# First cross-attention of a Perceiver-style network: the short key chunk moved from first to last, and the weighting dealt out in another rhythm

## The reference, cut to what matters

```python
q = (input_q @ wq).reshape(B, LQ, 16, 64).transpose(0, 2, 1, 3)     # LQ = 128
k = (input_k @ wk).reshape(B, LK, 16, 64).transpose(0, 2, 1, 3)     # LK = 12544
v = (input_k @ wv).reshape(B, LK, 16, 16).transpose(0, 2, 1, 3)
attn = softmax(einsum('bhqd,bhkd->bhqk', q, k) / sqrt(64), axis=-1)
out = einsum('bhqk,bhkd->bhqd', attn, v)                            # x = x + out
```

## Time and profile before

| | |
|---|---|
| median of 3 runs | 954.5 us (953.8 to 955.16) |
| the profiled execution, its own time | 958.71 us |
| its span, first to last instruction | 956.9 us |
| mean granted TensorE clock | 0.989 |
| TensorE busy | 925.9 us, 97% |
| VectorE, ScalarE, GpSimd busy | 73%, 60%, 39% |

### The profile page before, as it was taken

The page is one execution under the profiler, slowest core; times in us unless marked ns, Lnnn a source line. Parts: engine busy times, 40 slices in busy tenths (PEclk is TensorE's granted clock), DMA queues, the critical chain, the costliest instruction groups (busy, mean ns, idle before and its releaser), DMA issues.

```text
span 956.9 us, 30568 instructions
## 1 busy us (share of the span) xinstructions
PE 925.9 (97%) x13321; PEld 723.9 (76%) x13321; DVE 695.4 (73%) x876; ACT 570.2 (60%) x1404; POOL 372.8 (39%) x406
## 2 busy tenths in 40 slices
PE   7999999999999999999999999878989999999998
PEld 5667777777777777777777777567978887889998
DVE  4588888888888888888888888845035654367886
ACT  5666666666666666666666666503246663346764
POOL 2544444444444444444444444302023331513332
PEclk9999999999999999999999999979989999999999
DMA  6101101100101101000101100069449897409992
GB/s 237 25 25 25 25 25 25 25 25 25 25 25 25 25 26 25 25 25 25 25 25 25 25 3 3 3 257 382 138 176 274 283 281 274 174 2 313 323 335 92
DMA packets 78554, 98.10 MB, mean 103 GB/s; under 512 B 21584, under 2 KB 56928, under 8 KB 78432
## 3 DMA queue, kind: packets, MB, share of 16 engines
q1 hardware_dynamic: 77344, 94.67, 30.6%
q10 hardware_dynamic: 1088, 1.57, 0.5%
HBM read 95.68 MB, written 0.13 MB: 100 GB/s over the span
## 4 chain that ended last, share of the span: by engine, by line
PE 81%; DVE 7%; ACT 5%; issue 4%; POOL 2%; DMA 1%; SPq 0%; DVEq 0%; POOLq 0%
PE ps L360 28%; PE ps L411 18%; PE ps L421 9%; PE ps L369 7%; PE ps L1586 6%; PE ps L1062 3%; PE ps L1603 2%; PE ps L1607 2%; PE ps L1604 2%; ACT x_pr L1228 2%; DVE c1T_lo L1266 1%; DVE x_negc L1272 1%; ACT c1T_hi L1222 1%; DVE x_negm L1275 1%; ACT x_prT L1236 1%
## 5 line engine op out<-in xcount | busy, mean ns | idle before, releaser
L671 DVE TENSOR_REDUCE x_peak<-ps 128x2 f32<-128x1024 f32 (+1 forms) x200 | 239.5, 1205 | 90.3 <-PE ps L411 81.8
L587 ACT ACTIVATE probs<-ps,x_peak 128x512 f32<-128x512 f32 (+1 forms) x400 | 265.5, 693 | 49.8 <-DVE x_peak L671 49.5
L690 DVE STREAM_TRANSPOSE probsT<-probs 128x1024 f32<-128x1024 f32 (+1 forms) x200 | 225.5, 1183 | 2.8 <-ACT probs L587 2.8
L411 PE MATMUL ps<-keys,qT 64*32 64x512 f32 (+1 forms) x3200 | 216.9, 586 | 1.3 <-ACT probs L587 0.7
L574 ACT COPY keys<-ps 128x512 f32<-128x512 f32 (+1 forms) x200 | 113.3, 580 | 149.9 <-PE ps L360 149.9
L421 PEld LDWEIGHTS ps<-probsT,vals 64*32 64x32 f32 x6016 | 115.3, 106 | 94.0 <-issue 93.2
L859 POOL TENSOR_SCALAR vals<-vals_t,x_side 128x512 f32<-128x512 f32 (+1 forms) x100 | 151.9, 1536 | 51.6 <-PEq L429 51.6
L360 PE MATMUL ps<-ctxT_hi,wk_hi 128*128 128x512 f32 (+1 forms) x400 | 157.3, 393 | 0.0
L360 PE MATMUL ps<-ctxT_hi,wk_lo 128*128 128x512 f32 (+1 forms) x400 | 154.2, 386 | 0.0
L360 PE MATMUL ps<-ctxT_lo,wk_hi 128*128 128x512 f32 (+1 forms) x400 | 154.2, 386 | 0.0
L421 PE MATMUL ps<-probsT,vals 64*32 64x128 f32 x6016 | 131.9, 271 | 0.0
(11 more groups left out here) (252 smaller groups left out, 1304.8 us busy)
## 6 DMA issues: line engine op xcount, KB each, us to landing
m_w<-in_m_w SPq DMA_DIRECT2D x32, 1024.0 KB, 7.7
ctx_raw<-in_ctxT SPq DMA_DIRECT2D x24, 512.0 KB, 3.7
ctx_two<-in_ctxT SPq DMA_DIRECT2D x24, 512.0 KB, 4.3
ctx_one<-in_ctx SPq DMA_DIRECT2D x24, 512.0 KB, 5.5
x_shrinkT<-x_shrink SPq DMA_DIRECT2D x384, 1.0 KB, 1.7
f_h1T<-in_f_h1T SPq DMA_DIRECT2D x1, 4096.0 KB, 18.7
f_h2T<-in_f_h2T SPq DMA_DIRECT2D x1, 4096.0 KB, 26.0
m_shared_w<-in_m_sw SPq DMA_DIRECT2D x2, 1024.0 KB, 8.0
```

Source lines behind the costliest of these rows:

```text
L411: i = pe.matmul(m.ps[32 * j:32 * (j + 1), score_bank(t) + odd, 0:nt * P], m.qT[rows, 4 * group + j, qs], m.keys[rows, 4 * group + j, 0:nt ...
L587: return act.activation(m.probs[t][:, odd, 0:nt * P], m.ps[:, score_bank(t) + odd, 0:nt * P], ACT.Exp, bias=m.peak[slot][:, 1, 2 * (t // H ...
L671: dv.tensor_reduce(m.peak[slot][:, 1, cs, t % HALF], m.ps[:, bank:bank + 2, 0:nt * P], AX.X, ALU.min).then_inc(s["dve" if t == STEPS - 1 e ...
L690: i = dv.transpose(m.probsT[:, cs, 0:4 * nt, t % HALF * 32:t % HALF * 32 + 32], m.probs[t][:, :, 0:nt * P].rearrange("p c (b k) -> p c b k ...
```

## The change

The tail goes to the end, the steps deal the blocks out as 3, 2, 3, 2, 2, 2, 2, 0, and `x0_read` stands behind the second half of the last weighting. The calls get the sizes of the chunk and of the next one as arguments. The core of the diff:

```diff
-BLOCK_CUTS = (0, 2, 4, 6, 8, 10, 13, 15, 16)
+BLOCK_CUTS = (0, 3, 5, 8, 10, 12, 14, 16, 16)
...
-            blocks = range(BLOCK_CUTS[t] * of // BLOCKS, BLOCK_CUTS[t + 1] * of // BLOCKS)
+            blocks = range(BLOCK_CUTS[t], BLOCK_CUTS[t + 1])
             if len(blocks):
-                weighted(1 - slot, blocks, of)
+                weighted(1 - slot, blocks)
         if ahead:
             context_free(ahead)
-            wide(1 - slot, CHUNK_TILES)
+            wide(1 - slot, nt_next)
...
         pe.wait_ge(s["probs_turned"], n("probs_turned"))
-        pe.sem_inc(s["x0_read"], 1)
         pe.wait_ge(s["last_kept"], 1)
         last_weighted(slot, 2, nt)
+        pe.sem_inc(s["x0_read"], 1)
...
-    first_chunk(TAIL_TILES)
-    chunk(1, TAIL_TILES, (4, 2, 0), 2)
-    for i in range(N_FULL - 1):
-        chunk(i % 2, CHUNK_TILES, (2, 2, 2), max(0, min(2, N_FULL - 2 - i)))
-    last_output(0, CHUNK_TILES)
+    first_chunk(CHUNK_TILES)
+    chunk(1, (4, 2, 0), 2)
+    for i in range(N_FULL - 3):
+        chunk(i % 2, (2, 2, 2), 2)
+    chunk(1, (2, 2, 2), 1, nt_next=TAIL_TILES)
+    chunk(0, (2, 2, 2), 0, nt=TAIL_TILES)
+    last_output(0, TAIL_TILES)
...
-    act.dma_start(m.raw[0][:, :, 0:TAIL], columns[:, :, 0:TAIL]).then_inc(s["raw0"], 16)
+    act.dma_start(m.raw[0][:, :, :], columns[:, :, 0:CHUNK]).then_inc(s["raw0"], 16)
```

More of the change, by code:

```diff
@@ L421, in weighted @@
                     i = pe.matmul(m.ps[32 * c:32 * (c + 1), OUT_BANK + two, 0:P], m.vals[slot][rows, b, c, :],
-                                  m.probsT[rows, c, b, :], start=(b == 0), stop=(b == of - 1),
+                                  m.probsT[rows, c, b, :], start=(b == 0), stop=(b == BLOCKS - 1),
                                   skip_group_check=True)
-        if blocks[-1] == of - 1:
+        if blocks[-1] == BLOCKS - 1:
             i.then_inc(s["out_full"], 1)
@@ L434, in context_free, with chunk @@
             pe.sem_inc(s["raw_free"], 1)
-    def chunk(slot, nt_before, kept, ahead):
-        of = 4 * nt_before
+    def chunk(slot, kept, ahead, nt=CHUNK_TILES, nt_next=CHUNK_TILES):
         for t in range(STEPS):
@@ L443, in chunk @@
                 pe.wait_ge(s["probs_ready"], n("probs_ready"))
-            scores(t, CHUNK_TILES)
+            scores(t, nt)
             if t == 0:
@@ L653, in xattn0_scalar @@
     with act.Fori(0, (N_FULL - 4) // 2):
-        chunk(0, True)
-        chunk(1, True)
+        chunk(0, CHUNK_TILES)
+        chunk(1, CHUNK_TILES)
         n.restart(act, s, *looped)
-    chunk(0, True)
-    chunk(1, False)
-    chunk(0, False, "alpha_last")
+    chunk(0, TAIL_TILES)
+    chunk(1, 0, TAIL_TILES)
+    for t in range(STEPS):
+        exponentials(0, t, TAIL_TILES)
+    shrink_factors(0, "alpha_last")
     for half in range(2):
@@ L705, in turn_out, with chunk @@
                      ).then_inc(s["out_kept"], 1)
-    def chunk(slot, order, last=False):
+    def chunk(slot, order, nt=CHUNK_TILES, nt_next=CHUNK_TILES):
         if order >= 2:
@@ L712, in chunk @@
         for t in range(STEPS):
-            maxima(slot, t, CHUNK_TILES)
+            maxima(slot, t, nt)
         turn_out()
         for t in range(STEPS):
-            turn_probabilities(t, CHUNK_TILES, (HALF - 1, STEPS - 1) if last else (STEPS - 1,))
-            if t == HALF and not last:
+            turn_probabilities(t, nt, (STEPS - 1,) if nt_next else (HALF - 1, STEPS - 1))
+            if t == HALF and nt_next:
                 for half in range(2):
-                    turn_values(1 - slot, half, CHUNK_TILES, OUT_BANK + half)
+                    turn_values(1 - slot, half, nt_next, OUT_BANK + half)
     def split_key_weights(half):
@@ L794, in xattn0_vector @@
     layer_norm_vector(dv, m, s, n, m.x[0][:, :])
-    first_chunk(TAIL_TILES)
+    first_chunk(CHUNK_TILES)
     chunk(1, 1)
-    for _ in range((N_FULL - 2) // 2):
+    for _ in range((N_FULL - 4) // 2):
         chunk(0, 2)
         chunk(1, 2)
-    chunk(0, 2, True)
+    chunk(0, 2)
+    chunk(1, 2, nt_next=TAIL_TILES)
+    chunk(0, 2, TAIL_TILES, 0)
     last_factors(0)
@@ L862, in set_aside, with chunk @@
             t.then_inc(s["vals_ready"], 1)
-    def chunk(slot, split, signal="acc_added"):
+    def chunk(slot, nt_split, signal="acc_added", nt=CHUNK_TILES):
         for half in range(2):
-            set_aside(slot, half, CHUNK_TILES)
+            set_aside(slot, half, nt)
         rescale(1 - slot)
         add_out(1 - slot, signal)
-        if split:
+        if nt_split:
             for k in range(DK):
-                split_context(slot, k)
+                split_context(slot, k, nt_split)
     def first_chunk(nt):
```

61 lines of the change are left out of this document (31 added, 30 removed).

## The result

| | before | after |
|---|---|---|
| median of 14 runs each | 954.69 us (953.49 to 956.03) | 959.2 us (955.39 to 961.89) |
| ratio, 95% interval | | 1.0044 (1.0035 to 1.0054) |
| the profiled execution, its span | 958.71, 956.9 us | 956.6, 954.8 us |
| mean granted TensorE clock of the runs | | 0.995 in 4 runs (median 956.4), 0.986 to 0.991 in 10 (959.7) |

The change is slower by 0.4%, where 0.5% faster was forecast (949.3 us). The two profiled executions have it the other way round, by 2.1 us: the one of before was slow for its kernel, the one of after quick. Profiles of a second execution of each kernel are therefore used as well; they lie near the medians (954.25 and 959.67).

What follows compares the result with a forecast made beforehand. TensorE, busy 97% of the span, was taken as the bound, with ScalarE pacing steps 3 to 5 and VectorE the end. Terms from +10.1 to -6.4 summed to -5.2 us, giving 949.3 us, range 944 to 956.

Steps and rivals of the forecast that it cites:

- start: Start of the kernel: the first chunk, twice as wide, makes the first call begin later, +10.1 us.
- rhythm: Steps of the steady calls: blocks dealt 3, 2, 3, 2, 2, 2, 2, 0 save 0.17 us a call, -3.6 us.
- before the last call: Wide phase ahead of the last call: half as wide, but VectorE doesn't follow, so -2.7 us.
- last call, with its clock: Last call, first maximum to last turning: narrower work saves 6.4 us, TensorE's lower clock costs 2.2.
- last weighting to `x_odd`: Last weighting: fewer matmul records in its second half and no 2.80 us stall after moving the signal, -3.9 us.
- spare products to the next projection: Spare products ahead of the next transposes: half of up to 1.8 us saved if the clock is back, -0.9 us.
- calls of 24.69 us or more: Sign of being wrong, in the steady calls; calls of 24.5 us were expected.
- third rival: Last weighting: the 2.80 us stall stays or moves to other work on the path, total -2.4 us, 952.1; chance 0.12.
- The rhythm gives nothing: Rival on the steps: ScalarE sets the pace however blocks are dealt, total -1.6 us, 952.9; chance 0.11.
- The +2.2 for the idle stretch ahead of the last call: Last call: about 5 us of new TensorE idle time ahead of it lowers the clock, +2.2 us, bounds 0 to +4.

Runs made afterwards that it cites:

- the merged kernels: Kernel before with one product per head group for all blocks of a step: 948.64 us (0.9941) with new cuts, 952.44 us (0.9980) with old.
- cuts alone: Kernel before with only BLOCK_CUTS changed, to 3, 2, 3, 2, 2, 2, 2, 0: 954.12 us, ratio 1.0001.
- order alone and filled: Kernel before with only the chunk order changed (256 keys last), plus spare products in both idle TensorE stretches at the end: ratio 0.9997.
- each pair with the order: The whole change with either `x0_read` ahead again (order and cuts) or the old cuts (order and signal), against the kernel before: 1.0022 and 1.0019.

## Why the prediction was wrong, step by step

The terms of the sum, against the profiles of the two second executions (spans 952.4 and 957.9 us):

| term | forecast | measured |
|---|---|---|
| start | +10.1 | +9.4 (40.57 to 50.02; +11.4 between the first profiles) |
| rhythm, calls 1 to 22 | -3.6 | +1.2 |
| before the last call | -2.7 | -3.4 |
| last call, with its clock | -4.2 | -4.5 |
| last weighting to `x_odd` | -3.9 | +0.6 |
| spare products to the next projection | -0.9 | +2.4 |
| sum (the rest is -0.3) | -5.2 | +5.4 |

The start, the wait before the last call and the last call came out near their forecasts and within their bounds. By the signs that the prediction itself gave for being wrong, one came true: calls of 24.69 us or more. Three steps failed: the saving on the last weighting, the rhythm, and the price of the clock behind the last turnings.

*The signal and the last weighting, and the spare products.* The 2.80 us gap and the 6.08 us of spare products belonged to one execution. The shown median, 954.5, said that this execution lost 4.2 us to something, and I took these 4.2 off the base and counted the same time once more as a gain of 3.7 (2.8 for the stall, 0.9 for the spare products). The mechanism that I read into it, instructions late beside the burst of loads, fits that execution: its packet took 2.4 us and not 1.0, and the gap is at the packet border. What failed is taking it for a cost of every execution: the gap at that place is 0.33 us in the second profile, and moving the signal alone gave 1.0003. The third rival, the stall goes elsewhere, had named this place but with a gain kept. One reading was wrong beside this: TensorE was not without work in the turnings, the first half of the last weighting ran in them from 624.62; nothing in the sum hangs on it.

*The rhythm.* 24.49 us and 10.65 for a clean call are as worked out (24.5, 10.68), and the merged kernels show the 3.6 us. What failed is the tacit premise that a filled step stays filled: of calls 1 to 22, 8 to 10 take over 24.6 us in each profile, most with the gaps at packet borders. A part of the +1.2 is the order's and not the rhythm's: with the old cuts these calls take 543.3 to 544.3 us in the new order and 543.0 in the old one, with the new cuts in the old order 541.8. "The rhythm gives nothing" was right in its number (cuts alone: 1.0001) and wrong in its reason: not ScalarE but TensorE's own instructions. The Trainium skill has the packets (Runtime: NRT & Kernel Launch, section Instruction fetch mechanics): 16 KiB blocks of 256 instructions, fetched while the ones before run, at a cost mostly hidden. The size agrees with the 105 packets; "mostly hidden" held in the calls of the kernel before and not in those where 256 small instructions last about 3.5 us.

*The clock behind the last turnings.* The +2.2 for the idle stretch ahead of the last call has the right sign and is too large rather than too small: with the old cuts, filling it made that call 0.9 to 1.5 us shorter (14.4, against 14.2 worked out without the clock). But the second stretch, in the last turnings, had no price at all, and I let the spare products behind it gain 0.9 because the clock might be back; they and the way to the next projection lost 2.4. It is this stretch that decides, 3.2 us. In the kernel before, the low level began at 621 and at 623 in the two profiles, while TensorE was still idle, and was over before the second half of the last weighting; in the new order it begins within 2 us of the start of the whole last weighting and, in four of the six profiles where this stretch is not filled, lasts until 639 to 643, through the fold and the spare products. The Trainium skill's rule that idle gaps between bursts put TensorE back (TensorE: Matmul & The Clock Gate, section Why this matters for your kernels) agrees with both stretches by the windows, 0.50 at 618 and at 632; it does not say what that costs, which hangs on the work behind.

The price of the order by itself is then start +10.4 on a mean of the two pairs of profiles, and as much gained at the end once both stretches are filled: order alone and filled is 0.9997. Two things stay open. Which calls stall is not explained by the place of the border alone. And the three parts together (1.0044, 1.0039) cost more than their sum (1.0028), and each pair with the order has 1.0019 to 1.0022; the intervals overlap, and no run here separates chance in the clock from a real joint effect.

## What to carry to other kernels

Take a second profile of the base before a stall of one execution becomes a term of the sum, above all where its own time lies off the median of the runs. Where an engine is made to run small instructions without a pause, count the instructions per us beside the busy time: here steps with 256 in 3.6 us (10.84 us for 768) ran almost without gaps, and steps planned at 3.5 us did not. Before work is moved to the end of a phase, look where the engine's idle stretches will lie against its work behind them; a few spare products in the last one were worth 3.2 us.

## What the runs showed of the hardware

- TensorE's instructions come in packets of about 256; in stretches where 256 of them last about 3.5 us it stands for 0.35 to 0.95 us at packet borders (up to 1.54 in the last call), in some calls and not in others with the same layout. Cutting the steps of a call from 768 instructions to 480 ended it.
- A packet that came while the big loads ran took 2.4 us where the median is 1.0, and TensorE stood for 2.80 us.
- A separate semaphore increment in TensorE's stream takes 0.15 us from one to the next: 130 of them made a wide phase of 13.8 us last 19.5, though the products ran beside them.
- After the idle stretch of 4.1 us the granted clock was at the lower level for a time that differs between executions of one kernel: back by 635 in one, not before 642 in another.
